# Four output banks, spread query rows and a split gather in a four-layer gated network (fp32, one core)

## What is computed

```python
x = x + tanh(g_xattn[0]) * graph(ctx, norm(x))       # top 153 of 512 similarities per row
x = x + tanh(g_ffn[0]) * (fwht(silu(n @ W1.T) * (n @ W3.T)) @ W2.T)        # n = norm(x), hidden 2048
x = x + tanh(g_xattn[1]) * softmax(ln(sim))          # layer 1
x = x + tanh(g_ffn[1]) * thought_network(norm(x))
x = x + tanh(g_xattn[2]) * grouped(norm(x), ctx)     # 32 query heads of 16, 8 key/value heads
x = x + tanh(g_ffn[2]) * experts(norm(x))            # 8 experts, the best 2 of each row
x = x + tanh(g_xattn[3]) * latent(norm(x), ctx)      # 16 heads, rotated queries of 384
x = x + tanh(g_ffn[3]) * ((silu(n @ Wg.T) * (n @ Wu.T)) @ Wd.T)            # hidden 2048
```

## Time and profile before

| | |
|---|---|
| median of 3 timed runs | 4484.85 us (4482.78 to 4489.41) |
| the profiled execution | 4486.73 us, its span 4485.0 us |
| mean granted clock of TensorE | 0.923 |
| TensorE busy | 3742.6 us (83%) |
| VectorE busy | 2221.7 us (50%) |
| ScalarE busy | 1204.9 us (27%) |
| GpSimd busy | 363.3 us (8%) |
| mean DMA rate | 65 GB/s |

### The profile page before, as it was taken

The page is one execution under the profiler, slowest core; times in us unless marked ns, Lnnn a source line. Parts: engine busy times, 40 slices in busy tenths (PEclk is TensorE's granted clock), DMA queues, the critical chain, the costliest instruction groups (busy, mean ns, idle before and its releaser), DMA issues.

```text
span 4485.0 us, 38317 instructions
## 1 busy us (share of the span) xinstructions
PE 3742.6 (83%) x11794; PEld 1726.6 (38%) x11795; DVE 2221.7 (50%) x3419; ACT 1204.9 (27%) x2333; POOL 363.3 (8%) x388
## 2 busy tenths in 40 slices
PE   2198989884475888937994899999999998999999
PEld 0043434342142444414562344444444443444443
DVE  7787878316365766621113566566665563111111
ACT  1101010013032666612221334434344332001010
POOL 6000000000002222122113000000000000000000
PEclk6599999996786999968997999999999999999999
DMA  2221212130004434234555000000000001222221
GB/s 90 81 75 53 74 56 71 56 123 37 3 0 76 66 50 63 25 142 129 162 164 204 32 32 22 32 32 32 31 22 32 32 22 45 73 80 84 68 87 51
DMA packets 77498, 292.25 MB, mean 65 GB/s; under 512 B 10440, under 2 KB 11336, under 8 KB 66252
## 3 DMA queue, kind: packets, MB, share of 16 engines
q1 hardware_dynamic: 69072, 265.17, 20.1%
q0 software_dynamic: 8320, 25.71, 1.8%
HBM read 256.73 MB, written 33.59 MB: 65 GB/s over the span
## 4 chain that ended last, share of the span: by engine, by line
PE 61%; issue 22%; DVE 7%; DMA 4%; POOL 3%; ACT 2%; SPq 1%; DVEq 0%; POOLq 0%; ACTq 0%
PE BM L338 6%; PE BR L338 6%; PE BS L349 6%; PE BM L1721 5%; PE BM L1772 5%; PE BR L1780 4%; PE BS L1756 3%; PE BM L1731 2%; PE BT L1059 2%; PE BR L1414 2%; PE BM L1403 2%; PE BR L1403 2%; PE BT L1765 2%; PE BM L1745 2%; PE BS L1049 2%
## 5 line engine op out<-in xcount | busy, mean ns | idle before, releaser
L349 PE MATMUL BS<-AR 128*128 128x512 f32 x1024 | 452.8, 595 | 31.9 <-DVE X L393 31.9
L338 PE MATMUL BM<-XT,AR 128*128 (+1 forms) x1024 | 462.8, 595 | 11.9 <-ACT XT L238 5.5
L338 PE MATMUL BR<-XT,AR 128*128 (+1 forms) x1024 | 460.3, 592 | 0.0
L385 DVE TENSOR_TENSOR AR<-AR,BR 128x512 f32<-128x512 f32 x128 | 87.9, 687 | 506.0 <-PE BR L338 494.9
L1944 DVE SCALAR_TENSOR_TENSOR X<-BR,AR,X 128x512 f32<-128x512 f32 x256 | 192.0, 750 | 230.7 <-PE BR L1780 221.4
L1831 ACT COPY AR<-BM 128x512 f32<-128x512 f32 x340 | 199.4, 587 | 397.4 <-PE BM L1772 182.3
L349 PEld LDWEIGHTS BS<-AR 128*128 128x128 f32 x1024 | 191.9, 190 | 287.5 <-issue 229.6
L366 ACT ACTIVATE AR<-BM 128x512 f32<-128x512 f32 x128 | 76.4, 597 | 833.5 <-PE BM L338 833.4
L338 PEld LDWEIGHTS BM<-XT,AR 128*128 128x128 f32 x1024 | 194.5, 191 | 258.3 <-issue 258.3
L338 PEld LDWEIGHTS BR<-XT,AR 128*128 128x128 f32 x1024 | 194.6, 190 | 244.9 <-issue 244.9
L1837 ACT ACTIVATE AR<-BS,AR 128x512 f32<-128x512 f32 x256 | 175.6, 690 | 411.1 <-DVE AR L1931 411.1
(11 more groups left out here) (304 smaller groups left out, 5095.1 us busy)
## 6 DMA issues: line engine op xcount, KB each, us to landing
AR<-l_w_dram SPq DMA_DIRECT2D x128, 512.0 KB, 3.5
AR<-l_wq_dram SPq DMA_DIRECT2D x32, 1152.0 KB, 5.1
AR<-l_w_dram SPq DMA_DIRECT2D x42, 768.0 KB, 4.8
AR<-w2h SPq DMA_DIRECT2D x16, 1024.0 KB, 4.8
QS<-qx SPq DMA_DIRECT2D x32, 512.0 KB, 17.8
AR<-l_w_dram SPq DMA_DIRECT2D x16, 1024.0 KB, 4.8
AR<-l_w_dram SPq DMA_DIRECT2D x8, 1408.0 KB
made<-AR SPq DMA_DIRECT2D x40, 256.0 KB, 4.8
```

Source lines behind the costliest of these rows:

```text
L338: last = nc.tensor.matmul(bank.rearrange("p (a n) -> p a n", a=1), w[:, kt, a, :], XT[:, ds(b & 1, 1), kt, :], start=kt == 0, stop=kt == K ...
L349: last = nc.tensor.matmul(bank, f.HIDDEN[:, u, st * P:(st + 1) * P], f.DOWN[:, u, :], start=u == 0, stop=u == f.units - 1)
```

## The change

It joins three edits.

1. **Rows of QS2 and KS2.** Combination j is loaded into rows j, j + 4, ..., j + 60 instead of 16 j to 16 j + 15, for queries and keys alike. Nothing else of layer 2 changes.
2. **Four banks.** The down products' two pairs use BS and BT: `S_BANKS`. The semaphores of the adds count four free banks. In the last network, and in the last batch of layer 0, the transposes of the next batch move between the up products and the down products of the batch's last group; since they use BT, the second pair waits for their copies. The batch loop of the last network runs three times and the last batch stands behind it, without norm; the store's loop is written out.
3. **Gather.** 8 of the 32 gathered results are added before the last attention, 12 are gathered by then. GpSimd gathers the other 20 at the start of its part of the last attention, as buffers come free, and VectorE adds four in each of pairs 0 to 5, between `sums` and the output adds. For this, YG's area is kept out of the attention's buffers (4 D columns), and the weights and positions get tensors of their own. PROBT3 shrinks to one buffer for both heads; the context product of head 0 moves ahead of the turn of head 1's probabilities, on TensorE, on ScalarE and in the table.

```diff
@@ -323,8 +323,10 @@
-def ffn_tensor_batch(pe, f, m, r, s, n_in, b):
-    with loop(pe, f.groups // f.per_turn, (m, f.units * f.per_turn), (r, f.units * f.per_turn),
+S_BANKS = [BS[:, 0, :], BS[:, 1, :], BT[:, 0, :], BT[:, 1, :]]
+def ffn_tensor_batch(pe, f, m, r, s, n_in, b, groups=4, between=None):
+    with loop(pe, groups, (m, f.units * f.per_turn), (r, f.units * f.per_turn),
@@ -338,9 +340,15 @@
+            if between:
+                between()
...
-                banks = [start_job(pe, f.s, s) for _ in range(2)]
+                if between and pair:
+                    pe.wait_ge(turn.free, T_PE.now() + 2)
+                pe.wait_ge(f.s.free, s.now() + 2)
+                s.step(2)
+                banks = S_BANKS[2 * pair:2 * pair + 2]
@@ -353,10 +361,11 @@
 def ffn_tensor(pe, f):
...
-    with loop(pe, B, (m, f.groups * f.units), (r, f.groups * f.units), (s, f.groups * ST), (n_in, f.groups), (T_PE, KT), (N_PE, 1)) as b:
-        hold(pe, turn.free, T_PE.now() + 2)
-        ffn_tensor_batch(pe, f, m, r, s, n_in, b)
-        norm_tensor(pe)
+    pe.wait_ge(turn.free, T_PE.now() + 2)
+    with loop(pe, B - 1, (m, f.groups * f.units), (r, f.groups * f.units), (s, f.groups * ST), (n_in, f.groups), (T_PE, KT), (N_PE, 1)) as b:
+        ffn_tensor_batch(pe, f, m, r, s, n_in, b, f.groups - 1)
+        ffn_tensor_batch(pe, f, m, r, s, n_in, b, 1, lambda: norm_tensor(pe))
+    ffn_tensor_batch(pe, f, m, r, s, n_in, B - 1)
...
 def ffn_scalar_batch(act, f, m, r):
@@ -369,9 +378,10 @@
 def ffn_scalar(act, f):
...
-    with loop(act, B, (m, f.groups * f.units), (r, f.groups * f.units), (T_ACT, KT)) as b:
+    with loop(act, B - 1, (m, f.groups * f.units), (r, f.groups * f.units), (T_ACT, KT)) as b:
...
+    ffn_scalar_batch(act, f, m, r)
...
 def ffn_vector_batch(v, f, m, r, s, b, between=None, extra=()):
@@ -388,21 +398,22 @@
-                bank = full(v, f.s, s)
+                v.wait_ge(f.s.full, s.step())
...
-                nc.vector.scalar_tensor_tensor(out=xb, in0=bank, scalar=f.scale(b, turn_ * f.per_turn + q, st), in1=xb,
+                nc.vector.scalar_tensor_tensor(out=xb, in0=S_BANKS[st], scalar=f.scale(b, turn_ * f.per_turn + q, st), in1=xb,
...
-    v.wait_ge(f.s.free, s.now() + 2)
+    v.wait_ge(f.s.free, s.now() + 4)
...
 def ffn_vector(v, f):
...
-    v.sem_inc(f.s.free, 2)
-    with loop(v, B, (m, f.groups * f.units), (r, f.groups * f.units), (s, f.groups * ST), (T_V, KT), (N_V, 1)) as b:
-        norm_vector(v, (b + 1) & 3)
+    v.sem_inc(f.s.free, 4)
+    with loop(v, B - 1, (m, f.groups * f.units), (r, f.groups * f.units), (s, f.groups * ST), (T_V, KT), (N_V, 1)) as b:
+        norm_vector(v, b + 1)
...
+    ffn_vector_batch(v, f, m, r, s, B - 1)
@@ -447,8 +458,8 @@
-    ffn_tensor_batch(pe, l0f, m, r, s, n_in, B - 1)
-    norm_tensor(pe)
+    ffn_tensor_batch(pe, l0f, m, r, s, n_in, B - 1, l0f.groups - 1)
+    ffn_tensor_batch(pe, l0f, m, r, s, n_in, B - 1, 1, lambda: norm_tensor(pe))
...
 def l0_scalar(act):
@@ -479,7 +490,7 @@
 def l0_vector(v):
...
-    v.sem_inc(l0f.s.free, 2)
+    v.sem_inc(l0f.s.free, 4)
@@ -964,12 +975,12 @@
     def keys(half, b):
...
-            sp.dma_start(KS2[16 * j:16 * j + 16, 4 * half:4 * half + 4, :].bitcast(F32),
+            sp.dma_start(KS2[j:64:4, 4 * half:4 * half + 4, :].bitcast(F32),
...
     def queries(half):
...
-            sp.dma_start(QS2[16 * j:16 * j + 16, 16 * half:16 * half + 16, :].bitcast(F32),
+            sp.dma_start(QS2[j:64:4, 16 * half:16 * half + 16, :].bitcast(F32),
...
     def maxima(n):
@@ -1310,8 +1321,10 @@
-MX0, MX1, MS, EX, WT0, WT1, POS0, POS1 = [a(B * ST) for _ in range(8)]
-IDX0, IDX1, YP0, YP1 = [a(B * ST).bitcast(I32) for _ in range(4)]
+MX0, MX1, MS, EX, POS0, POS1 = [a(B * ST) for _ in range(6)]
+IDX0, IDX1 = [a(B * ST).bitcast(I32) for _ in range(2)]
+WT0, WT1 = [sb(n, [P, B * ST])[:, :] for n in ("WT0", "WT1")]
+YP0, YP1 = [sb(n, [P, B * ST], I32)[:, :] for n in ("YP0", "YP1")]
@@ -1446,6 +1459,21 @@
+def moe_combine(v, k):
+    tile, j = divmod(k, 2)
+    v.wait_ge(yg_in[k % 4], 16 * (k // 4) + 16)
+    nc.vector.scalar_tensor_tensor(out=X[:, tile, :], in0=YG[k % 4], scalar=(WT0, WT1)[j][:, tile:tile + 1],
+                                   in1=X[:, tile, :], op0=ALU.mult, op1=ALU.add).then_inc(yg_used, 1)
+    v.wait_ge(yg_used, k + 1)
+def moe_gather(pool, k):
+    tile, j = divmod(k, 2)
+    if k >= 4:
+        pool.wait_ge(yg_used, k - 3)
+    nc.gpsimd.indirect_dma_start(out=YG[k % 4], out_offset=None, in_=made,
+                                 in_offset=bass.IndirectOffsetOnAxis(ap=(YP0, YP1)[j][:, tile:tile + 1], axis=0))\
+      .then_inc(yg_in[k % 4], 16)
 def moe_vector(v):
@@ -1539,12 +1567,8 @@
-    for k in range(2 * B * ST):
-        tile, j = divmod(k, 2)
-        v.wait_ge(yg_in[k % 4], 16 * (k // 4) + 16)
-        nc.vector.scalar_tensor_tensor(out=X[:, tile, :], in0=YG[k % 4], scalar=(WT0, WT1)[j][:, tile:tile + 1],
-                                       in1=X[:, tile, :], op0=ALU.mult, op1=ALU.add).then_inc(yg_used, 1)
-        v.wait_ge(yg_used, k + 1)
+    for k in range(8):
+        moe_combine(v, k)
@@ -1580,13 +1604,8 @@
-    for k in range(2 * B * ST):
-        tile, j = divmod(k, 2)
-        if k >= 4:
-            pool.wait_ge(yg_used, k - 3)
-        nc.gpsimd.indirect_dma_start(out=YG[k % 4], out_offset=None, in_=made,
-                                     in_offset=bass.IndirectOffsetOnAxis(ap=(YP0, YP1)[j][:, tile:tile + 1], axis=0))\
-          .then_inc(yg_in[k % 4], 16)
+    for k in range(12):
+        moe_gather(pool, k)
@@ -1616,11 +1635,11 @@
-a = area(E * KT * 2 * I + 2 * EK * D)
+a = area(E * KT * 2 * I + 2 * EK * D + 4 * D)
...
-PROB3, PROBT3 = [a(ST, S), a(ST, S)], [a(ST, S), a(ST, S)]
+PROB3, PROBT3 = [a(ST, S), a(ST, S)], a(ST, S)
@@ -1645,12 +1664,13 @@
+            if p >= 0 and h == 1:
+                put("m", "ctx", p, 0)
...
-            for h in range(2):
-                put("m", "ctx", p, h)
+            put("m", "ctx", p, 1)
@@ -1769,7 +1789,7 @@
-            last = nc.tensor.matmul(bank, KVN[:, p // 8 * ST + lt, :], PROBT3[h][:, lt, :], start=lt == 0, stop=lt == ST - 1)
+            last = nc.tensor.matmul(bank, KVN[:, p // 8 * ST + lt, :], PROBT3[:, lt, :], start=lt == 0, stop=lt == ST - 1)
...
     def outputs(p, h):
@@ -1812,9 +1832,10 @@
+            if h:
+                context(p, 0)
...
-        for h in range(2):
-            context(p, h)
+        context(p, 1)
@@ -1840,7 +1861,7 @@
     def probs(p, h, lt):
...
-        nc.scalar.copy(PROBT3[h][:, lt, :], BT[:, L3[job] % 2, :]).then_inc(t_free, 1)
+        nc.scalar.copy(PROBT3[:, lt, :], BT[:, L3[job] % 2, :]).then_inc(t_free, 1)
...
     def big(p, h, k):
@@ -1880,10 +1901,10 @@
+        take(("ctx", p, 0), CC3[0])
...
-        for h in range(2):
-            take(("ctx", p, h), CC3[h])
+        take(("ctx", p, 1), CC3[1])
@@ -1971,6 +1992,9 @@
+    def combine(k):
+        moe_combine(v, k)
@@ -1984,6 +2008,9 @@
+        if 8 + 4 * p < 2 * B * ST:
+            for k in range(8 + 4 * p, 12 + 4 * p):
+                combine(k)
@@ -1992,6 +2019,8 @@
 def l3_pool(pool):
+    for k in range(12, 2 * B * ST):
+        moe_gather(pool, k)
@@ -2090,10 +2119,11 @@
-    with loop(pool, B, (N_P, 1)) as b:
-        norm_pool(pool)
-        pool.wait_ge(x_done, b + (7 * B + 1))
-        nc.gpsimd.dma_start(out[ds(b * S, S), :].rearrange("(n p) d -> p n d", p=P), X[:, ds(b * ST, ST), :]).then_inc(stored, 16)
+    for b in range(B):
+        if b < B - 1:
+            norm_pool(pool)
+        pool.wait_ge(x_done, 7 * B + 1 + b)
+        nc.gpsimd.dma_start(out[b * S:(b + 1) * S, :].rearrange("(n p) d -> p n d", p=P), X[:, b * ST:(b + 1) * ST, :]).then_inc(stored, 16)
...
 def layouts(inp):
```

## The result

The changed kernel takes 4384.62 us (median of four runs, 4380.72 to 4385.36) against 4484.61: a ratio of 0.9774, 95% interval 0.9757 to 0.9791, 100 us faster. The profiled execution took 4384.69, its span is 4382.8. The gather's part saved 9 us more than its terms said; the largest of them that was wrong is the cost of the single buffer.

The account below looks back on a forecast made before the run. Idle time of TensorE, stage by stage, was taken to bound the kernel. From 4486.73 us profiled, -33.6 - 28.5 - 26.6 = -88.7 gave 4398.0 profiled, 4396 as a median, with a range of 4385 to 4418.

Parts of the forecast that it names:

- Part 1: Grouped attention: spread query rows load faster, saving 8.8 us at the start and 24.8 at three stalls, 33.6 in all.
- The 250 GB/s: Rate of 128-row stores just before the query load; taken as upper bound for spread rows, -9.2 us at the start.
- the doubling: Query load rate at the grouped attention's start doubles from 119 to 238 GB/s, saving 8.8 us.
- the later waits at each second load: Grouped attention: each batch's second load holds TensorE 1 to 3 us; ScalarE's casts come next, so no gain.
- Part 2: Gated networks: four output banks save 25.1 us in the last network and 3.4 in layer 0, 28.5 in all.
- Rival (c): Gated networks: the pause is not the bank's, so four banks don't help; 4421 us, chance 0.04.
- Part 3: Last attention: gathering one batch ahead saves 33 us, costs 6 for the buffer and 0.4 in pair 4: -26.6.
- the single buffer, at +6 us: Last attention: one buffer for turned probabilities makes TensorE wait longer in each of 32 pairs, 6 us more in all.
- the 0.18: Extra per pair of the last attention, 0.18 or 0.19 us: third turn waits 0.43 for 0.35, context product about 0.1.
- The bounds of 0 to 16: Range for the buffer's cost in the last attention: both waits as before, or 0.5 us in each of 32 pairs.
- -33 for the start: Ahead of the last attention: turn of batch 0 starts at 2423.3 instead of 2456.25; bounds -29 and -37 us.
- rival (d): Last attention: gathers beside VectorE work back on it, 8 us more, 4404; chance 0.04.

Follow-up runs that it names:

- the rows alone: Kernel before with only the key and query rows spread four apart: 4448.3 us against 4483.9, ratio 0.9917.
- the buffer alone: Kernel before with only one buffer for the turned probabilities and head 0's context product moved ahead: 4487.69 us against 4484.05, ratio 1.0006.
- the gather alone: Kernel before with only 8 results ahead, 24 inside the last attention and one buffer for turned probabilities: 4448.44 us against 4483.9, ratio 0.9919.
- the banks alone: Kernel before with only the four output banks and the norm's turn moved ahead: 4455.75 us against 4483.9, ratio 0.9939.

## Why the prediction was right, and where it was off

**Part 1: -33.6 forecast, -35.6 alone.** The mechanism holds: the old rows set the rate, the backlog was the stall, and all three stalls are gone whole: 8.74 + 8.87 + 7.80 = 25.4 for 24.8. (The bound of 26.2 counted the third stall as long as the first too; with only the second so long it is 25.3.) The start was mis-sized in two terms that nearly cancel. The rate in the middle of the load is 202 GB/s and not 238, so it gained 7.3 and not 8.8; the estimate of 218 from the page of the Trainium skill (SBUF — State Buffer, Door 1: The DMA port swizzle) was nearer. The 250 GB/s that I leaned on was a mean over two things, the end of the keys' slow load and the stores. Where, by the order of issue, the stores run by themselves, the kernel before moves 399:

```profile
1360.00:1364.00 4.00, 0.00 (x0) 0.00 (x0) 0.00 (x0) 0.00 (x0) 3.88 (x3) 0.50 1.03 399
```

So the store was no bound near 250 for these loads, and the doubling came out near by luck: nothing in the trace of before pointed to 1.7 times the old rate. And the sum had no term for the keys, loaded by the same rows ahead of the queries' store: the query load is issued 16.4 to 17.1 us after the context's load in every kernel with spread keys and 17.8 to 19.2 in the others, 1.8 us between before and after. That the later waits at each second load gain nothing holds within scatter: the three stretches of two steps over them take 108.7 us before, 106.2 after and 108.7 with the rows alone.

**Part 2: -28.5 forecast, -28.2 alone.** Groups of 41.20 where 41.22 was said, the boundary 2.48 where 2.5 was said, the last network 24.8 shorter where 25.1 was said, and the last batch of layer 0 1.9 shorter (173.15 us from the turn of its rows to layer 1's first load, for 175.02) where 1.9 was said. In layer 0's batches 0 to 2 the groups shrink from 42.44 to 41.20, but VectorE's search takes most of it back at the end of each: in batch 0 TensorE waits 8.24 us for it there instead of 4.89. From turn to turn the three are 0.7 shorter, 0.7 shorter and 1.0 longer, 0.4 in sum for the 1.5 that I had. The 1.0 can be scatter, since a batch with the code of before takes 203.2 or 204.5 us with the rows alone where others take some 201.5. Rival (c) is out.

**Part 3: -26.6 forecast, -35.5 alone.** Here is the step that failed: the single buffer, at +6 us. From the first output product to the last, the attention takes 1241.61 us before, 1242.88 with the buffer alone and 1242.74 in the changed kernel, so it costs about 1, and 0 in the gather alone (1241.80). A pair pays 0.09 and not 0.18. Of the two halves of the 0.18, the 0.1 for the context product that is moved up holds in size: from the start of each part to that of the next row are 3.54 and 3.43 us, 6.97 for the 6.87 in one piece. The other half, a wait of 0.43 instead of 0.35, is wrong: the wait is 0.29. I had set 1.4 us of ScalarE, for the context's copy and the first copy of probabilities, against 0.98 us of two transposes, as if the copy ahead were new. The kernel before already has a copy of 0.59 us in that place, of queries:

```profile
2592.61 1.04 PE L1765 MATMUL BT<-ID,AR 128*128 128x128 f32 x8
2592.86 0.59 ACT L1831 COPY AR<-BM 128x512 f32<-128x512 f32 x1 [0.27 <-PE BM L1731]
2593.34 1.08 ACT L1843 COPY AR<-BT 128x512 f32<-128x512 f32 x2
```

From the first two turns to the third it is 2593.99 - 2592.61 = 1.38 us there. In the changed kernel that copy is made beside the context product, the context's copy stands in its place and starts 0.06 us sooner behind the turn (0.19 for 0.25), and the distance is 2519.85 - 2518.53 = 1.32. And the last pair, where nothing of a next pair fills the waits, gains: the step to it is 37.4 to 38.9 us in the three kernels without this edit and 34.9 to 36.2 in ten with it. The bounds of 0 to 16 stood on one side only: nothing there let the reordering gain.

The other term, -33 for the start, was right for the part alone (48.19 instead of 81.68 from the first gather to the first query product, 33.5) and too small in the joined kernel (45.28, so 36.4; 44.9 to 46.8 in six more with the same code there). I had 1 us for the folded weights' loads; up to the context's turns 0.6 is gained in the part alone and 3.0 in the joined kernel (39.54 instead of 42.57), and why they differ stays open. The turn with its wait takes 3.15 instead of 4.43: TensorE no longer comes from 31.93 us of idle, and its granted clock over this turn is 1.00 instead of 0.59. The adds are hidden as said. The meeting with the norm's statistics in pair 4 costs 0.26 for 0.4 (40.12 for the 39.86 of the buffer alone). The 20 gathers beside the attention take 1099 ns to issue as a median, the 12 ahead 947; neither VectorE nor TensorE waits for them, so rival (d) is out.

**Luck.** The time left the range by 0.4 us, less than the scatter between runs, so that it lies outside and not just inside is chance. That it lies so low is not: had the buffer cost its 6 us, it would have been near 4390. The buffer, the start and the stalls came in near their low ends together, which the range had taken for unlikely, and two gains, at the keys and at the store, had no term.

**The rest** is a gain that I had at nothing: GpSimd issues the last store 0.5 us sooner (0.37 instead of 0.85 us behind the last add). The kernel with the banks alone shows it too, so it belongs to part 2, where the store's loop is written out and the last norm left away; which of the two does it isn't shown. The ledger closes, in the spans of the two traces: against the forecast's terms the attention is 5.7 shorter, its start 3.4, part 1's stage 2.8 and the store 0.5; layer 1 and the experts' network, which the edit doesn't touch, are 0.9 and 1.9 shorter in this trace, and 1.7 are missing in the gated networks. That is 13.5 between forecast and trace, 11.4 between forecast and median. Each entry carries the scatter of its stretch; of the attention's 5.7, the 5.3 between its first and last output product are beyond it.

## What to carry to other kernels

Before a moved copy is priced, look in the trace at what the engine does in that place today: if another copy moves out of the way, the moved one takes its place, and only what sticks out beyond it costs. A bound on a reordering has two sides, since it also moves work into gaps. And once a load is as fast as its rows allow, ask which bytes of it the first step needs.

## What the runs showed of the hardware

- 16 rows two apart are filled as fast as 16 rows four apart (184 GB/s over the whole load in both), 16 neighbours at 114.
- Issuing is slower for spread rows: eight key loads take 6.7 to 7.2 us on SP instead of 5.6 to 5.7, eight query loads 5.0 to 5.7 instead of 4.0 to 4.3. It lies beside the transfers here.
- Waits of 0.29 and 0.92 us, once in each pair of some 40 us, leave eight matmul records at 3.60 us. Coming from 31.93 us of idle, TensorE had a granted clock of 0.59 over its next 4.4 us.
- Stretches of the same code differ from trace to trace by up to 4 us (460.62 to 464.57 in fourteen traces) to 4.5 us (1316.18 to 1320.72 in six), and the grouped attention began between 1343.5 and 1351.2 in four kernels with the same layers 0 and 1. Effects of a few microseconds are to be read from distances that repeat, such as the pairs.
